# Turning x of the expert tile after the next, behind the down-projection, in a fused post-norm block

## The reference, cut to what matters

```python
logits = x @ gate_w.T
top_w, top_i = jax.lax.top_k(jax.nn.softmax(logits), 2)
top_w = top_w / jnp.sum(top_w, axis=-1, keepdims=True)
...
for e in range(12):
    h = jax.nn.silu(x @ w1[e].T) * (x @ w3[e].T)      # 320 wide
    out = out + h @ w2[e].T * cw[:, e:e + 1]
```

## Time and profile before

| | us |
|---|---|
| median of 3 runs | 766.68 (765.8 to 772.09) |
| profiled execution, its own time | 766.03 |
| its span, first to last instruction | 764.2 |
| PE busy in the span | 726.6 (95%) |
| DVE, ACT, POOL busy | 501.2, 346.3, 303.2 |

### The profile page before, as it was taken

The page is one execution under the profiler, slowest core; times in us unless marked ns, Lnnn a source line. Parts: engine busy times, 40 slices in busy tenths (PEclk is TensorE's granted clock), DMA queues, the critical chain, the costliest instruction groups (busy, mean ns, idle before and its releaser), DMA issues. The chain is left out here.

```text
span 764.2 us, 17944 instructions
## 1 busy us (share of the span) xinstructions
PE 726.6 (95%) x6231; PEld 523.6 (69%) x6232; DVE 501.2 (66%) x1102; ACT 346.3 (45%) x695; POOL 303.2 (40%) x336
## 2 busy tenths in 40 slices
PE   9999899999999999999999987999999999999994
PEld 4777677777877778787766866666666666666641
DVE  3857868878688686896878885444444444444477
ACT  3865654656456566686465212222222222222264
POOL 0564455463654645645411002343343433344310
PEclk9999899999999999999999999999999999999998
DMA  8824365353652545546310037255555555522955
GB/s 332 307 87 135 112 218 170 94 170 126 197 179 80 178 142 166 180 136 210 111 71 15 30 139 260 86 193 199 179 212 200 199 193 201 196 82 87 333 235 196
DMA packets 40123, 126.77 MB, mean 166 GB/s; under 512 B 4224, under 2 KB 4608, under 8 KB 38144
## 3 DMA queue, kind: packets, MB, share of 16 engines
q1 hardware_dynamic: 31024, 99.49, 37.5%
q0 software_dynamic: 6880, 22.55, 8.9%
q10 hardware_dynamic: 2160, 3.93, 1.4%
HBM read 81.13 MB, written 44.83 MB: 165 GB/s over the span
## 5 line engine op out<-in xcount | busy, mean ns | idle before, releaser
L1090 DVE COPY_PREDICATED ST<-msk,pS 128x256 f32<-128x256 uint8 x224 | 121.2, 570 | 58.0 <-issue 30.0
L765 POOL TENSOR_TENSOR piece_parts<-piece,piece_parts 128x1024 f16<-128x1024 f32 x48 | 103.9, 2166 | 100.4 <-ACT piece_parts L710 100.4
L1576 PE MATMUL pH<-ring,xgh 128*128 x344 | 103.2, 300 | 4.8 <-issue 3.8
L1577 PE MATMUL pH<-ring,xgh 128*128 x344 | 102.9, 299 | 0.0
L1578 PE MATMUL pH<-ring,xgl 128*128 x344 | 102.9, 299 | 0.0
L759 POOL TENSOR_TENSOR RL<-RL,AM 128x256 f32<-128x256 f32 x96 | 70.6, 736 | 79.5 <-ACT RL L702 71.8
L403 PE MATMUL pS<-RL 64*128 64x64 f32 (+2 forms) x1536 | 98.9, 267 | 0.0
L1789 DVE TENSOR_TENSOR hid<-pH,sil 128x320 f32<-128x320 f32 x43 | 21.1, 491 | 117.6 <-ACT sil L1660 117.6
L1888 POOL DMA_INDIRECT y_scratch<-ysb,sidx x43 | 42.7, 993 | 137.6 <-DVE ysb L1805 134.2
L403 PEld LDWEIGHTS pS<-RL 64*128 64x128 f32 (+1 forms) x1536 | 89.5, 178 | 4.3
L1660 ACT ACTIVATE sil<-pH 128x320 f32<-128x320 f32 x43 | 18.8, 437 | 129.0 <-PE pH L1578 129.0
(11 more groups left out here) (254 smaller groups left out, 1545.7 us busy)
## 6 DMA issues: line engine op xcount, KB each, us to landing
piece<-in_w_experts SPq DMA_DIRECT2D x48, 512.0 KB, 5.0
w_split_scratch<-piece_parts SPq DMA_DIRECT2D x48, 512.0 KB, 3.9
ring<-w_split_scratch SPq DMA_DIRECT2D x12, 2048.0 KB, 8.5
yin<-y_scratch SPq DMA_DIRECT2D x16, 512.0 KB, 12.9
out_x<-X SPq DMA_DIRECT2D x8, 512.0 KB, 2.8
x_scratch<-X ACTq DMA_DIRECT2D x15, 256.0 KB, 2.0
X<-in_x SPq DMA_DIRECT2D x2, 1536.0 KB, 18.1
RL<-in_wxT SPq DMA_DIRECT2D x4, 256.0 KB, 5.0
```

The lines of the kernel that those rows point to most:

```text
L765: g.tensor_tensor(piece_parts[buf][:, 1, :], piece[buf][:, :], piece_parts[buf][:, 0, :], ALU.subtract).then_inc(piece_lo, 1)
L1090: v.copy_predicated(out[:, :, :, 0 if lv == 0 else 1, :], msk[:, lv, :, :].rearrange(shape, m=m), pS[:, :, lv * S:(lv + 1) * S].rearrange( ...
L1576: pe.matmul(p[:, 0, 0:F], xgh[par][:, k, :], wh, start=(k == 0), stop=False)
L1577: pe.matmul(p[:, 0, 0:F], xgh[par][:, k, :], wl, start=False, stop=False)
```

## The change

TensorE's order becomes `hidden(i)`, `down(i - 1)`, `turn(i + 2)`, `turn_hidden(i)`: x is turned one tile further ahead, and behind the down-projection. The turns go alternately into `pX` and `pG` (the list `pXT`). ScalarE and VectorE follow with `high_x(i + 2)` and `low_x(i + 2)`; VectorE does `copy_out(i - 1)` before `low_x(i + 2)`. Three waits of TensorE go: `xt_out` in `turn`, `hid_out` in `hidden`, `o_out` in `down`. The register load of the place for `down(i - 1)` is made between the two halves of `hidden(i)`. Two tiles are turned ahead of the first `hidden`. GpSimd's program and the number of buffers stay as they are.

```diff
--- before.py
+++ after.py
@@ -1407,6 +1407,7 @@
         pHT = ps("pHT")
         pO = ps("pO")
         pMix = [pX, pG, pH1, pH3, pHT]
+        pXT = [pX, pG]
 
         dv = sem("dv")
         gate_T = sem("gate_T")
@@ -1552,24 +1553,30 @@
 
                 buf = k % AHEAD
                 pe.wait_ge(x_in[buf], rounds * 16)
-                pe.wait_ge(xt_out, i + 1)
-                for k in range(KT):
-                    t = pe.transpose(pX[:, 0, k * P:(k + 1) * P], xg[buf][:, k * P:(k + 1) * P], idt[:, :])
+                for kt in range(KT):
+                    t = pe.transpose(pXT[k % 2][:, 0, kt * P:(kt + 1) * P], xg[buf][:, kt * P:(kt + 1) * P], idt[:, :])
                 t.then_inc(xt_full, 1)
 
             def weights(slot, rows, at, n):
 
                 return [ring[0:rows, bass.ds(slot, 1), u, at:at + n].rearrange("p o n -> p (o n)") for u in range(2)]
 
-            def hidden(i, par):
+            def place(i):
+
+                return nc.values_load(tabi[0:1, 1, bass.ds(i, 1)], engines=PE, min_val=0, max_val=RING - 1,
+                                      skip_runtime_bounds_check_because="a place in the ring")
+
+            def hidden(i, par, former=None):
 
                 need, slot = [nc.values_load(tabi[0:1, k, bass.ds(i, 1)], engines=PE, min_val=lo, max_val=hi,
                                              skip_runtime_bounds_check_because="an expert's number or place")
                               for k, lo, hi in ((0, 1, E), (1, 0, RING - 1))]
                 pe.wait_ge(w_ready, need)
                 pe.wait_ge(xt_out, i + 2)
-                pe.wait_ge(hid_out, i + 1)
+                held = None
                 for n, p in ((0, pH1), (1, pH3)):
+                    if n and former is not None:
+                        held = place(former)
                     for k in range(KT):
                         at = k * 2 * F + n * F
                         wh, wl = weights(slot, P, at, F)
@@ -1577,6 +1584,7 @@
                         pe.matmul(p[:, 0, 0:F], xgh[par][:, k, :], wl, start=False, stop=False)
                         t = pe.matmul(p[:, 0, 0:F], xgl[par][:, k, :], wh, start=False, stop=(k == KT - 1))
                 t.then_inc(h_full, 1)
+                return held
 
             def turn_hidden(i):
                 pe.wait_ge(hid_out, i + 2)
@@ -1584,11 +1592,8 @@
                     t = pe.transpose(pHT[:, 0, k * P:(k + 1) * P], hid[:, k * P:(k + 1) * P], idt[:, :])
                 t.then_inc(ht_full, 1)
 
-            def down(i):
-                slot = nc.values_load(tabi[0:1, 1, bass.ds(i, 1)], engines=PE, min_val=0, max_val=RING - 1,
-                                      skip_runtime_bounds_check_because="a place in the ring")
+            def down(i, slot):
                 pe.wait_ge(ht_out, i + 1)
-                pe.wait_ge(o_out, i + 1)
                 for k in range(FT):
                     wh, wl = weights(slot, P, KT * 2 * F + k * C, C)
                     pe.matmul(pO[:, 0, :], hTh[:, k, :], wh, start=(k == 0), stop=False)
@@ -1601,25 +1606,25 @@
 
             pe.wait_ge(table_ready, 1)
             turn(0, 0, 1)
-            busy(5)
+            turn(1, 1, 1)
+            busy(3)
             hidden(0, 0)
-            turn(1, 1, 1)
+            turn(2, 2, 1)
             turn_hidden(0)
 
             def tile(i, k, rounds=None):
 
-                hidden(i, k % 2)
+                down(i - 1, hidden(i, k % 2, i - 1))
                 if rounds is not None:
-                    turn(i + 1, k + 1, rounds)
-                down(i - 1)
+                    turn(i + 2, k + 2, rounds)
                 turn_hidden(i)
-            rounds = (SLOTS - 2) // AHEAD
+            rounds = (SLOTS - 3) // AHEAD
             with pe.Fori(0, rounds) as j:
                 for k in range(1, AHEAD + 1):
-                    tile(j * AHEAD + k, k, j + ((k + 1) // AHEAD + 1))
+                    tile(j * AHEAD + k, k, j + ((k + 2) // AHEAD + 1))
             for i in range(rounds * AHEAD + 1, SLOTS):
-                tile(i, i % AHEAD, (i + 1) // AHEAD + 1 if i + 1 < SLOTS else None)
-            down(SLOTS - 1)
+                tile(i, i % AHEAD, (i + 2) // AHEAD + 1 if i + 2 < SLOTS else None)
+            down(SLOTS - 1, place(SLOTS - 1))
             for u, i in enumerate(ON_PE):
                 pe.wait_ge(y_in[i], 16)
                 pe.wait_ge(diag_ready, u + 1)
@@ -1649,7 +1654,7 @@
 
             def high_x(i, par):
                 a.wait_ge(xt_full, i + 1)
-                a.copy(xgh[par][:, :, :], pX[:, 0, :].rearrange("p (k t) -> p k t", k=KT)).then_inc(xg_hi, 1)
+                a.copy(xgh[par][:, :, :], pXT[par][:, 0, :].rearrange("p (k t) -> p k t", k=KT)).then_inc(xg_hi, 1)
 
             def high_hidden(i):
                 a.wait_ge(ht_full, i + 1)
@@ -1662,17 +1667,18 @@
             def tile(i, k, more=True):
                 silu(i)
                 if more:
-                    high_x(i + 1, (k + 1) % 2)
+                    high_x(i + 2, k)
                 high_hidden(i)
             high_x(0, 0)
+            high_x(1, 1)
             tile(0, 0)
             tile(1, 1)
-            pairs = (SLOTS - 1) // 2
+            pairs = (SLOTS - 2) // 2
             with a.Fori(1, pairs) as j:
                 tile(j * 2, 0)
                 tile(j * 2 + 1, 1)
             for i in range(pairs * 2, SLOTS):
-                tile(i, i % 2, more=i + 1 < SLOTS)
+                tile(i, i % 2, more=i + 2 < SLOTS)
 
             a.wait_ge(wtop_ready, 1)
 
@@ -1791,7 +1797,7 @@
 
             def low_x(i, par):
                 v.wait_ge(xg_hi, i + 1)
-                v.tensor_tensor(xgl[par][:, :, :], pX[:, 0, :].rearrange("p (k t) -> p k t", k=KT), xgh[par][:, :, :],
+                v.tensor_tensor(xgl[par][:, :, :], pXT[par][:, 0, :].rearrange("p (k t) -> p k t", k=KT), xgh[par][:, :, :],
                                 ALU.subtract).then_inc(xt_out, 1)
 
             def low_hidden(i):
@@ -1807,20 +1813,21 @@
             def tile(i, j, k, more=True):
 
                 gate(i)
-                if more:
-                    low_x(i + 1, (k + 1) % 2)
                 if j is not None:
                     copy_out(i - 1, j, (k + 1) % 2)
+                if more:
+                    low_x(i + 2, k)
                 low_hidden(i)
             low_x(0, 0)
+            low_x(1, 1)
             tile(0, None, 0)
             tile(1, 0, 1)
-            pairs = (SLOTS - 1) // 2
+            pairs = (SLOTS - 2) // 2
             with v.Fori(1, pairs) as j:
                 tile(j * 2, j - 1, 0)
                 tile(j * 2 + 1, j, 1)
             for i in range(pairs * 2, SLOTS):
-                tile(i, (i - 1) // 2, i % 2, more=i + 1 < SLOTS)
+                tile(i, (i - 1) // 2, i % 2, more=i + 2 < SLOTS)
             copy_out(SLOTS - 1, (SLOTS - 1) // 2, (SLOTS - 1) % 2)
 
             def terms(q):
```

## The result

The changed kernel takes 826.57 us (median of four runs, 823.44 to 830.64); the kernel before took 767.29 us in its four. The ratio is 1.077 with a 95% interval of 1.071 to 1.083, so the change makes the kernel 7.7% slower. The forecast was 816 us, with a range of 797 to 828. The profiled execution took 830.64 us, its span is 828.8 us.

The account below looks back on a forecast made before the run. TensorE's work (5.76 us a tile) and the chain through the register loads (5.84 to 5.87) were taken as nearly equal bounds. Double steps of 13.4 us, single steps, slowed gathers and branches summed to 291.2 against 240.8: 816 us, range 797 to 828.

Parts of the forecast that it names:

- My own case: Whole kernel: late x, slowed gathers and held register loads at full clock give 808 to 824 us; chance 0.66.
- rival C: TensorE's clock falls behind long waits for x, some three stretches, +4 to +12 us, 820 to 828 us; chance 0.10.
- A sequencer makes no register load behind an unfulfilled wait: TensorE's sequencer: the next hidden's loads wait for x, so landing to hidden takes 1.15 us.
- Rival A: Register loads not held up by the wait for x: 0.81 us from landing to hidden, 808 us; chance 0.08.
- Waits removed: TensorE's load chain: only dropping the wait for hid_out wins, 0.09 us for each of 41 tiles, 3.7 us.
- Alternating banks, place read earlier, prologue: Two banks for turn, down's register load inside hidden, two turns ahead of the first hidden: 0 us each.
- x is 1.5 us late, and a step of two tiles is 13.4 us: At the moved turn x lands 1.5 us late, so two tiles take 13.4 us where two pitches took 12.04.
- The slowed gathers: Gathers beside weight or result loads each add 2.5 us or more; ten on the path, 26.5 us.
- The sum without the clock: Longest path from tile 1 to 41 at full clock: 291.2 us against 240.8, giving 816 us in all.
- The clock: TensorE's durations were taken at the full clock; a fall was only a rival, +4 to +12 us, chance 0.10.
- What would show it: Signs in the changed chain: gather in nearly every tile, pitches alternating about 5.75 and 7.7, mean 7.2 us.
- Rival D: x lands in time, leaving the shorter load chain, 3.7 us, and 1.3 us of present waits: 761 us; chance 0.03.

Follow-up runs that it names:

- a_hoist: Changed kernel with the two register loads of the next tile's hidden made ahead of the wait for x in three of four tiles; 823.69 us, ratio 1.077.
- b_gather_nowait: Kernel before with each gather issued ahead of the scatter and without TensorE's waits for hid_out and o_out; 758.88 us, ratio 0.991.
- a_gather: Changed kernel with GpSimd issuing the gather of tile i + 4 ahead of the scatter of tile i; 757.43 us, ratio 0.990.
- a_noring: Changed kernel without the nine loads of experts' weights within the loop, every matmul kept; 801.42 us, ratio 1.047.
- b_gather: Kernel before with GpSimd issuing the gather of tile i + 4 ahead of the scatter of tile i; 762.81 us, ratio 0.998.
- a_rotated: Changed kernel with gather ahead of scatter and TensorE's loop turned so register loads and branch precede the wait for hid; 751.80 us, ratio 0.982.
- a_filler: Changed kernel with eight idle 128x128 matmuls between the down-projection and the turn of every tile; 836.45 us, ratio 1.094.
- a_infront: Changed kernel with the turn of tile i + 2 put back in front of down(i - 1), gathers still late; 993.02 us, ratio 1.300.

## Why the prediction was right, and where it was not

The forecast was 816 us and 826.57 were measured, 1.4 us inside the upper end of the range. My own case, 808 to 824, does not reach it: that the time is inside is owed to what the range allowed for rival C.

*A sequencer makes no register load behind an unfulfilled wait*: right for these loads. The changed kernel's stand 0.2 us behind the landing, a_hoist's 3 us ahead of it, and landing to hidden is 1.18 us against 0.87 (1.15 and 0.81 forecast). Rival A is out.

The Trainium skill, "Perfetto Trace Analysis", section "Tensor Engine Instruction (MATMUL, LD_WEIGHTS)", has the sequencer free for the next instruction once the waiting one is in the wait queue. The traces here disagree where that next instruction is a register load: 487.1 behind the landing at 486.91.

*Waits removed, 0.09 us a tile, 3.7 us*: right, 3.6 us in b_gather_nowait.

*Alternating banks, place read earlier, prologue, each 0*: right within what these runs tell. a_gather's pitches are the engine's own work of 5.76 us, so nothing of the three shows there.

*x is 1.5 us late, and a step of two tiles is 13.4 us*: right. x was 1.3 us late in the first such tile, and in a_noring the step measured 13.35 to 13.38 us, 13.83 over a branch.

*The slowed gathers*: right. Without those of the weight loads the sum gives some 800 us (the 797 of prompt gathers and 3 for the last two), and a_noring took 801.4. In the changed kernel's chain nine gathers took 5.8 to 7.1 us, 23 us more than nine of 3.5 would; the sum had ten of them and 26.5 us.

*The sum without the clock*: 816 us forecast, 818 by the estimate above when brought to before's clock.

*The clock*: this is the step that failed. The sum took TensorE's durations at the full clock, and the fall was a rival with a chance of 0.10. It came in every run of the changed kernel (0.972 to 0.982 of the clock), nine times within the tiles of the profiled one, also behind waits of some 2 us, where I had allowed for about three stretches. Its price, some 9 us, is what rival C had, and the time is where C put it, 820 to 828 us. C had three stretches for 4 to 12 us, where nine cost some 9: the count too low, the price of each too high. The row that should have raised its chance was there: an idle of 3.7 us followed by half clock, and the sum itself forecast three waits of that length, so that "no fall" was the case that needed a reason.

*What would show it*: partly wrong. I wrote that the gather would stand in the chain in nearly every tile; by the forecast's own step of two tiles it had to be about every second one, and so it is: 18 gathers in 40 tiles. The mean pitch was put at 7.2 us and is 7.6, mostly by the clock as estimated above.

*Rival D, x in time, 761 us*: a_gather is this case, 757.4 us. I had the 3.7 us of the wait, and valued the waits for late x at 1.3 us; b_gather shows 2.6 us in the tiles for them.

## What to carry to other kernels

When a consumer is moved ahead, write down the whole loop of its data through every engine and queue, with the buffer's release and the order in which the issuing engine does its other work. Here the gather stood behind a scatter that waited for the very down-projection behind which the turn was put; the whole loss was bought back by swapping two calls on GpSimd.

Two waits that were always fulfilled cost 0.09 us a tile here, 3.6 us in 40 tiles, where the sequencer was the last link. Register loads and a branch behind an unfulfilled wait lengthen the step by what no work of the engine covers; putting both ahead of it gave another 4.0 us (a_gather to a_rotated, 234.0 to 230.0).

Where a forecast has TensorE wait for some two microseconds or more, price tiles behind these waits at half clock too. Not every such wait brings a fall: here nine came with 24 waits.

## What the runs showed of the hardware

A gather of 256 KB issued in the loop mostly took 3.2 to 3.5 us from the start of its issue to landing, in all kernels, and 5.5 to 7.1 us when it was issued 3.3 to 3.4 us behind the start of a weight load of 2 MB. Where the gathers were issued a tile earlier (b_gather_nowait, a_rotated) those of other tiles met the loads and were as slow, 5.7 to 6.9 us.

TensorE's granted clock fell within the tiles of the changed kernel, whose matmuls waited 24 times for x, 4.5 us at most (0.95 over 305.6 us), and a little in a_noring with 21 waits of 2.0 us at most (0.99 over 277.5 us); with no wait for x above 0.7 us (a_filler) it did not fall in any tile. A microsecond more at 1.2 GHz went with 0.36 to 0.43 us more of time, between runs of one kernel. A TensorE that waited in every tile (a_infront) had 0.79 of the clock over 466 us.

An fp32 matmul of 128x128 by 128 columns that is not a transpose held TensorE for 0.22 us (eight in 1.79 us, a_filler), twice the 0.11 of a transpose of the same size.
